# Unread identity products placed in TensorE's waits, in an attention, expert, linear-attention and coupling kernel

## The reference

```
h = layernorm(x) * (1 + ca) + sa
x = x + ga * causal_softmax_attention(h)      # 16 heads of 16, one shared k and v head, rotary
h = layernorm(x) * (1 + cb) + sb
x = x + gb * experts(h)                       # 16 experts, each takes its top 64 tokens of every sequence
h = layernorm(x) * (1 + ca') + sa'            # second block, its own modulation
x = x + ga' * linear_attention(h)             # elu+1 features, cumulative sums, causal
h = layernorm(x) * (1 + cb') + sb'
x = x + gb' * coupling(h)                     # three cycles of a small network
```

## Time and profile before

| | us |
|---|---|
| median of 3 runs | 1191.42 |
| the runs | 1188.3, 1191.42, 1193.76 |
| the profiled execution, whole | 1191.18 |
| its span in the trace | 1189.4 |

### The profile page before, as it was taken

The page is one execution under the profiler, slowest core; times in us unless marked ns, Lnnn a source line. Parts: engine busy times, 40 slices in busy tenths (PEclk is TensorE's granted clock), DMA queues, the critical chain, the costliest instruction groups (busy, mean ns, idle before and its releaser), DMA issues. The chain is left out here.

```text
span 1189.4 us, 19798 instructions
## 1 busy us (share of the span) xinstructions
PE 1070.3 (90%) x6630; PEld 603.6 (51%) x6630; DVE 733.1 (62%) x1549; ACT 596.0 (50%) x1133; POOL 465.7 (39%) x692
## 2 busy tenths in 40 slices
PE   5499999999999998479999865999999998999996
PEld 3244554454454543346656432556666674455554
DVE  2667878787787783624333323767777781665665
ACT  3167677676766666013333324534444435866732
POOL 2444635444453511068888873333333310000000
PEclk9599999999999999579999987999999998999988
DMA  3522415233241411436676771011211002001001
GB/s 133 112 46 29 82 29 99 63 70 77 57 93 32 73 39 59 150 107 137 165 158 137 178 136 32 6 60 41 77 41 41 19 20 89 1 27 56 25 27 45
DMA packets 73685, 85.31 MB, mean 72 GB/s; under 512 B 12577, under 2 KB 67817, under 8 KB 73457
## 3 DMA queue, kind: packets, MB, share of 16 engines
q1 hardware_dynamic: 61296, 67.27, 21.6%
q0 software_dynamic: 12288, 16.79, 8.2%
HBM read 45.58 MB, written 25.47 MB: 60 GB/s over the span
## 5 line engine op out<-in xcount | busy, mean ns | idle before, releaser
L560 DVE TENSOR_REDUCE nmax<-psum 128x1 f32<-128x512 f32 (+3 forms) x352 | 215.6, 637 | 44.9 <-PE psum L779 39.7
L677 ACT ACTIVATE pT<-psum 128x512 f32<-128x512 f32 x320 | 181.1, 596 | 65.6 <-PE psum L800 35.6
L777 PE MATMUL psum<-k6T,q6T 96*128 96x512 bf16 (+3 forms) x512 | 128.2, 310 | 17.8 <-DVE nmax L560 14.0
L797 PE MATMUL psum<-q6T,k6T 99*128 99x512 bf16 x320 | 119.4, 382 | 1.1 <-ACT pT L677 0.9
L1085 POOL DMA_INDIRECT residual<-expert_y,idx_e x64 | 101.0, 1578 | 22.0 <-issue 16.5
L777 PEld LDWEIGHTS psum<-k6T,q6T 96*128 96x128 bf16 x512 | 45.7, 99 | 91.6 <-DVE nmax L560 59.1
L1604 DVE TENSOR_TENSOR l_scores<-psum,const_sb 128x512 f32<-128x512 f32 x128 | 79.5, 684 | 20.3 <-PE psum L1779 20.3
L779 PE MATMUL psum<-negs_bf,ident_bf 128*128 128x128 bf16 (+2 forms) x352 | 88.8, 252 | 0.0
L812 PE MATMUL psum<-pT,v 128*32 128x512 f32 x640 | 85.0, 604 | 0.0
L1072 POOL DMA_INDIRECT expert_tokens<-router_input,idx_e x64 | 62.7, 980 | 52.4 <-POOLq L903 33.2
L1737 PE MATMUL psum<-l_hT,l_w 128*128 128x512 f32 x128 | 63.7, 621 | 0.8 <-ACT l_plus_one L1681 0.8
(11 more groups left out here) (298 smaller groups left out, 2220.5 us busy)
## 6 DMA issues: line engine op xcount, KB each, us to landing
q6T<-q_parts SPq DMA_DIRECT2D x96, 128.0 KB, 4.5
expert_w<-in_ew SPq DMA_DIRECT2D x16, 768.0 KB, 4.8
x_in<-in_x SPq DMA_DIRECT2D x8, 512.0 KB, 4.3
residual<-x SPq DMA_DIRECT2D x32, 128.0 KB, 1.9
router_input<-h SPq DMA_DIRECT2D x32, 128.0 KB, 1.8
l_x<-residual SPq DMA_DIRECT2D x8, 512.0 KB, 4.3
x_dram<-l_x SPq DMA_DIRECT2D x32, 128.0 KB, 1.7
out<-c_out SPq DMA_DIRECT2D x16, 256.0 KB, 2.1
```

The source lines that it names most:

```text
L560: dve.tensor_reduce(nmax[:, i, u * nh:(u + 1) * nh], ps_s[:, n % SR, 0:nh * (i + 1) * P].rearrange("p (h k) -> p h k", h=nh), AX_X, ALU.ma ...
L677: act.activation(pT[:, n % PR].rearrange("p h t -> p (h t)"), ps_t[:, n % TR, :], ACT.Exp, scale=HD ** -0.5).then_inc(probs, 1)
L777: pe.matmul(out[:, a, :], q6T[0:6 * HD, b % 2, u * nh + a, i * P:(i + 1) * P], k6T[0:6 * HD, b % 2, 0:w], start=a == 0, stop=False, skip_g ...
L797: last = pe.matmul(out, k6T[:, b % 2, j * P:(j + 1) * P], q6T[:, b % 2, hg * 4:hg * 4 + 4, i * P:(i + 1) * P], start=True, stop=j < i)
```

## The change

A function `keep_active` issues `count` products of the bf16 identity with itself, broadcast to 512 columns, into a PSUM bank that is free at that point. Nobody reads the result. It is called in six places: 14 products ahead of `kT` of sequence 0, 18 at the first scores of sequence 0 with heads 8 to 15, 16 at the start of routing, 6 after the modulation products, 12 after the transposes of indices and values, and 40 after the last expert. At the scores the wait for `s_max` moves ahead of the waits for `x_drain` and `q_placed`.

```diff
+def keep_active(pe, m, bank, count):
+    moving = m.ident_bf[:].unsqueeze(1).to_broadcast([P, NT, P])
+    for _ in range(count):
+        pe.matmul(bank.rearrange("p (n k) -> p n k", k=P), m.ident_bf[:], moving, start=True, stop=True, skip_group_check=True)
...
                         if b == 0:
                             pe.wait_ge(ready, 2)
+                            keep_active(pe, m, px, 14)
                         pe.wait_ge(k6_ready, b + 1)
...
                         nh, n = S_HEADS[i], s_use[s]
+                        if n >= SR:
+                            pe.wait_ge(s_max, n - SR + 1)
                         if first_scores[b, u * nh // 8] == s:
+                            if b == 0 and u:
+                                keep_active(pe, m, ps_s[:, n % SR, :], 18)
                             pe.wait_ge(x_drain, x_use[("kT", b)] + 1)
                             pe.wait_ge(q_placed[b % 2][u * nh // 8], 96 * (b // 2 + 1))
-                        if n >= SR:
-                            pe.wait_ge(s_max, n - SR + 1)
...
             def _(pe):
 
+                keep_active(pe, m, m.psum[:, 4, :], 16)
                 pe.wait_ge(mod_loaded, 16)
...
                 last.then_inc(mod_fill, 1)
+                keep_active(pe, m, m.psum[:, 4, :], 6)
                 pe.wait_ge(tables, 1)
...
                 pe.transpose(m.psum[:, 1, 0:P], vals[:].rearrange("p r s -> p (r s)"), ident).then_inc(turned, 1)
+                keep_active(pe, m, m.psum[:, 4, :], 12)
...
                                   start=False, stop=True, skip_group_check=True).then_inc(l3_fill, 1)
+                keep_active(pe, m, ps_t[:, 0, :], 40)
```

## The result

The changed kernel takes 1192.82 us (median of 20 runs, 1189.39 to 1196.22). The kernel before, timed in turn with it, takes 1188.82 (20 runs, 1183.16 to 1193.76). The ratio is 1.0034 [1.0023, 1.0045], that is +4.0 us (+2.7 to +5.4): slower, but within 0.5%. The forecast was 1198.3, +7.1 us, with a range from 1193.5. Part of that is the base: the forecast started from the one profiled execution, 1191.18, which is 2.4 us above the median of twenty.

What follows compares the result with a forecast made beforehand. PE was taken to bound mid-attention, DVE routing and POOL the experts. Terms 0 + 4.6 + 0 + 0.2 + 2.3 + 0 = 7.1 us on the profiled 1191.18 gave 1198.3 us, range 1193.5 to 1202.

Steps and rivals of the forecast that it cites:

- Places 4 and 5: Routing's 6 and 12 products: transposes 0.2 us late, then PE's drain moves the barrier by 2.3 us, bounds 0.3 to 3.3.
- 4.5 to 5 us after 503.3: In routing: when the clock would rise during the 12 products, so that they end at about 508.5.
- Place 1: Ahead of kT: 14 products make it 0.7 to 2.0 us late, covered by DVE's 5.29 us input wait; cost 0.
- Place 2: First scores, heads 8 to 15: 18 products behind the long wait take 5.5 us; net +4.6, bounds 2.5 and 7.4.
- the 0.9 assumed: First scores: about 0.5 us back from the former half-clock stretch and about 0.4 from PE's idle time.
- No give-back in attention: Attention after the first scores: with PE at 98% busy, nothing gives the filler's delay back.
- Place 3: Start of routing: 16 products take 6.9 us at most, hidden by the wmod DMA landing at 490.8; cost 0.
- Does it buy a warm first expert? So 0.: First expert: clock falls before its dense products, gain 0; had it held, first layer 3.60 instead of 5.88 us.
- Place 6: After the experts: 40 products end at 712.9, barrier stays at 721.8, clock falls by about 716.5; no cost, no gain.
- Identity products don't lift the clock: Rival, 8%: the fillers leave the clock low, the first scores cost 7.4 us and routing 3.3, giving 1201.9.
- Hidden at routing: Rival, 12%: clock up through 503 to 506, so routing's fillers cost only 0.3 us; 4.6 + 0.3 gives 1196.1.
- Carried clock: Rival, 12%: full clock lasts over the stage changes, gaining 2.3 us in experts and 3.8 in linear; 1190.0, not slower.

Runs made afterwards that it cites:

- the second profile: The changed kernel run again, unaltered, against the kernel before on another chip: 1197.57 against 1190.94 us, ratio 1.0046.

## Why the prediction was wrong, and what of it held

The mechanism held: a filler behind the wait costs, one under another wait doesn't, and PE's drain moves routing's barrier. What failed are sizes. The forecast was 5.5 us above the measured 1192.82. Of that 2.4 us are the base, 1191.18 where twenty runs give 1188.82. The other 3.1 are the sum, 7.1 against +4.0: place 2 was 0.6 too large and routing 1.1, and up to 1.2 came back at the first expert where the sum had 0. The rest is within the interval.

- **Places 4 and 5, forecast 0.2 + 2.3, measured +1.4. This is the step that failed.** It is the count of the clock's rise, "4.5 to 5 us after 503.3". The clock rose only 0.8 us after the first transpose in the profile of after, 0.5 to 3.4 us in the four profiles with both places, and 2.8 and 4.0 in the two with place 5 alone. The twelve then took 2.8 to 4.2 us and not 4.6 to 5.1. Two things were missing. Dense work begins with place 4, 2.5 to 2.9 us ahead of the transposes, and I had priced place 4 only as a delay: I had the pieces in two paragraphs and did not lay them end to end. And the distance itself scatters, 2.8 to 5.9 us from the start of the dense stretch over seven profiles; my own rows said "three to over five", and I took 4.5 to 5. Which of the two weighs more stays open.
- **The base.** One execution stood for the kernel, and the range gave three runs no spread of their own. With 1188.82 the forecast would have been 1195.9.
- **Place 1, forecast 0.** Held: kT 1.64 us late, inside the 0.7 to 2.0, covered by the input's wait, which was still 6.82 us. In the second profile the clock was full there, which I had not considered, and kT wasn't late.
- **Place 2, forecast +4.6, measured +4.0** (3.2 in the profile of after), and +4.3 (2.6 to 6.0) for the kernel with it alone. The step that carried it was to find out from the timeline which S step the condition picks: the one behind the long wait. The filler's 5.5 us were measured at 5.01, 6.19 and 6.08. What came back was more than the 0.9 assumed: 5.76 on average less 4.0 is 1.8.
- **No give-back in attention.** Held to within 0.4 us: 417.0 us from that Q to the end before, 417.1 after.
- **Place 3, forecast 0.** Held: 485.02 to 491.5, while the DMA came at 494.2. L956 took the same 8.70 us.
- **"Does it buy a warm first expert? So 0."** The clock was down at the expert's start, as forecast, but rose sooner: the first layer took 4.64 us, not 5.88, and POOL's wait shrank by 1.26. I had let it be either warm or not. That the filler did it isn't shown, since a profile without places 4 and 5 has 4.61.
- **Place 6, forecast 0.** Held, on both counts.
- **The sum.** With the measured terms 4.0 + 1.4 - (0 to 1.2) = 4.2 to 5.4, against +4.0 (2.7 to 5.4) and +5.5 (3.3 to 7.6) measured.
- **The rivals.** "Identity products don't lift the clock" is out: 48 of them took 11.66 us, 0.24 each, and 80 took 17.43, 0.22 each. "Hidden at routing" (0.3) lies no farther from the measured 1.4 than the forecast's 2.5 does, and I had given it only 12%. "Carried clock" is out for this change. On the price of one product, the section "Back-to-back issue gap" of "TensorE: Matmul & The Clock Gate" of the Trainium skill has 131 ns for 512 columns in a stream; the runs differ, with 218 ns over 80 products.

What stays open: the kernel with all but place 2 was measured at +3.6 (+1.9 to +5.2), its stages show +2.1, and with place 2 alone it adds to more than the whole. Its parts measured by themselves, +1.7 for places 4 and 5 and +1.1 for places 1, 3 and 6, make 2.8, inside its interval. Places 1, 3 and 6 alone, at +1.1 (-1.0 to +3.2), don't decide whether one of them costs a microsecond late in the kernel, where single profiles differ by more than that.

## What to carry to other kernels

A filler that keeps the clock up is worth something only if it reaches, without a break, into dense work that is on the path; one that ends some microseconds early costs nothing and brings nothing, and one that stands behind the wait, with work ready, costs most of its length (4.0 of 5.8 us with 18 products, 8.6 of 10.4 with 36). PE's drain ahead of a barrier waited for its unread products too, so put none there unless another engine is later by more than they last. And price fillers in the order in which the engine meets them, since an earlier one may set the clock at which the later ones run, and with a range for the moment at which the clock rises, since here it moved by 3 us from profile to profile.

## What the runs showed of the hardware

**The clock's rise comes at no fixed distance.** In routing the granted clock rose 3.3, 5.8, 3.0 and 5.9 us after place 4's first product in the four profiles with both places, 3.7 us after it with place 4 alone, and 4.0 and 2.8 us after the first transpose with place 5 alone.

**A thin stretch loses the clock even if it was entered at full.** With 80 products PE's last filler ended at 724.9, two groups of transposes followed at full speed, and the clock fell at 728.2, ahead of the heavy products at 729.1. That is 3.3 us after the last filler, as far as it fell behind PE's last expert product in the earlier trace rows (3.4 us). The section "Part 4: PE-mode transpose" of the same page of the Trainium skill says that transposes don't engage the full clock. The trace agrees in part: these did not keep it, but while it was there they used it (0.63 against 1.08 us for four).

**Idle time put down to "remote".** On two of the chips ACT or DVE stood idle for 2.3 to 6.7 us about the first expert, in every kernel run there, and POOL's first adding DMA came 25.5 to 25.8 us after the barrier, whether the first layer took 3.67 or 5.97 us. On the others no such wait is in the trace, and the same distance is 21.5 to 23.7 us. A gain or a loss of 2 us at that place shows on some chips and not on others. What the engines wait for isn't shown; no experiment here touched it.
